# Padded weight tiles in a Mamba-style block: each slot of both projections at another byte offset from its matmul partner

## The reference

```
n    = layernorm(x)
proj = n @ in_proj_w.T               # 512 -> 8192 gates, 8192 hidden, 2*8*128 B and C, 128 dt
hBC  = silu(causal_conv4(hidden, B, C) + conv_b)
dt   = clip(softplus(dt + dt_bias));  A = -exp(A_log)
Y    = chunked state scan over 128 heads of 64, state 128, chunks of 128 tokens, + D * hs
g    = Y * silu(gate);  out = group_rmsnorm(g, 8 groups) * norm_w
x    = x + out @ out_proj_w.T        # 8192 -> 512
x    = x + layernorm(x) @ (W + sum_e probs_e B_e A_e).T + b
```

## The kernel before, in words

|---|---|
| `w_high`, `w_low` and `x_high`, `x_low` (input projection, last product) | 64 |
| `y_high`, `y_low` and `out_high`, `out_low` (output projection) | 0 |
| `wdt_high`, `wdt_low` and `x_high`, `x_low` (dt product of the prologue, L251 to L253) | 192 |
| `y_high` and `x_high` (the one weight load at the switch from L734 to L770) | 352 |

## Time and profile before

### The profile page before, as it was taken

How to read it: one execution, slowest core, us unless ns; L and a number is a source line. 1 busy time by engine, 2 the same in 40 slices (tenths; PEclk the granted TensorE clock), 3 DMA queues, 4 the chain that set the end, 5 groups by cost and what they waited for, 6 DMA issues and landing times.

```text
span 1849.7 us, 32321 instructions
## 1 busy us (share of the span) xinstructions
PE 1693.5 (92%) x9616; PEld 1372.8 (74%) x9616; DVE 1464.4 (79%) x2214; ACT 1186.5 (64%) x1627; POOL 1362.0 (74%) x933
## 2 busy tenths in 40 slices
PE   7789999899998989989899999989999898998989
PEld 4568778687777867777687777867777786777867
DVE  7695986959789595977959689695977959598695
ACT  5674865747667574866658577574856758477562
POOL 1494985949679494985949689494976949588594
PEclk9899999999999999999999999999999999999999
DMA  5542432423344242433434344342433334243231
GB/s 205 198 134 79 159 117 101 132 78 136 107 131 137 83 128 82 154 113 102 136 110 152 102 131 138 94 118 95 140 113 113 123 100 128 89 151 117 94 103 46
DMA packets 121876, 220.40 MB, mean 119 GB/s; under 512 B 30176, under 2 KB 46560, under 8 KB 121312
## 3 DMA queue, kind: packets, MB, share of 16 engines
q1 hardware_dynamic: 121824, 219.76, 37.1%
HBM read 212.88 MB, written 6.82 MB: 119 GB/s over the span
## 4 chain that ended last, share of the span: by engine, by line
POOL 43%; PE 32%; issue 19%; DVE 2%; ACT 1%; POOLq 0%; DVEq 0%; ACTq 0%
POOL w_low L1219 11%; POOL square_sum L1225 8%; POOL scores L1245 8%; POOL xdecay L1264 8%; POOL y L1231 7%; PE bank L770 6%; PE bank L772 6%; PE bank L771 6%; POOL out_low L1254 3%; PE bank L732 3%; PE bank L733 2%; PE bank L734 2%; PE bank L809 1%; PE bank L869 1%; DVE scores L1115 1%
## 5 line engine op out<-in xcount | busy, mean ns | idle before, releaser
L1219 POOL TENSOR_TENSOR w_low<-raw,w_high 128x512 fp32r<-128x512 f32 x285 | 399.6, 1402 | 390.2 <-DVE scores L1115 312.7
L732 PE MATMUL bank<-x_high,w_high 128*128 128x512 f32 x1140 | 484.5, 425 | 6.3 <-POOL w_low L1219 4.1
L733 PE MATMUL bank<-x_low,w_high 128*128 128x512 f32 x1140 | 457.1, 401 | 0.0
L734 PE MATMUL bank<-x_high,w_low 128*128 128x512 f32 x1140 | 455.5, 400 | 0.0
L1019 DVE SCALAR_TENSOR_TENSOR hs<-bank,cols,hs 128x511 f32<-128x511 f32 x381 | 280.7, 737 | 40.1 <-ACT hs L896 40.0
L732 PEld LDWEIGHTS bank<-x_high,w_high 128*128 128x128 f32 x1140 | 219.8, 193 | 73.6 <-issue 31.5
L734 PEld LDWEIGHTS bank<-x_high,w_low 128*128 128x128 f32 x1140 | 218.6, 192 | 53.4
L733 PEld LDWEIGHTS bank<-x_low,w_high 128*128 128x128 f32 x1140 | 220.6, 193 | 41.7
L1033 DVE TENSOR_TENSOR scores<-scores,bc 128x1024 f32<-128x1024 f32 x128 | 242.1, 1891 | 3.7 <-ACT bc L994 3.7
L1264 POOL TENSOR_TENSOR xdecay<-xdt,tables 128x384 f32<-128x384 f32 x128 | 215.7, 1685 | 37.1 <-DVE xdt L1150 37.1
L905 ACT ACTIVATE w_high<-raw 128x512 fp32r<-128x512 f32 x285 | 177.2, 622 | 97.8 <-PE bank L734 90.9
(11 more groups left out here) (135 smaller groups left out, 2933.2 us busy)
## 6 DMA issues: line engine op xcount, KB each, us to landing
raw<-w_in SPq DMA_DIRECT2D x288, 256.0 KB, 2.7
sums<-sums_dram SPq DMA_DIRECT2D x128, 512.0 KB, 3.7
out_raw<-w_out SPq DMA_DIRECT2D x128, 256.0 KB, 3.6
grown_rows<-grown_dram SPq DMA_DIRECT2D x256, 96.0 KB, 3.4
xt<-x SPq DMA_DIRECT2D x8, 256.0 KB, 5.0
mixed<-x SPq DMA_DIRECT2D x2, 1024.0 KB, 7.6
table_dram<-table SPq DMA_DIRECT2D x2, 768.0 KB, 3.7
tables<-table_dram SPq DMA_DIRECT2D x32, 48.0 KB, 2.1
```

The costliest lines, as they stand in the source:

```text
L732: pe.matmul(to[:], w_high[:, slot, k], x_high[:, b, k], start=(k == 0), stop=False)
L733: pe.matmul(to[:], w_high[:, slot, k], x_low[:, b, k], start=False, stop=False)
L734: mm = pe.matmul(to[:], w_low[:, slot, k], x_high[:, b, k], start=False, stop=(k == KT - 1))
L1219: pool.tensor_tensor(w_low[:, t % SPLIT], raw[:, t % RAW], w_high[:, t % SPLIT].bitcast(F32), ALU.subtract).then_inc(w_low_ready, 1)
```

## The change

The tile `w_high` gets 448 bytes in front of it (an unused tile) and 160 bytes of padding behind each of its 3 slots; `w_low` gets 32 bytes in front and the same padding. Each of the 8 slots of `out_high` and `out_low` gets 64 bytes of padding. No instruction is added, removed or moved, and no operand changes its shape; only addresses change. All that is allocated behind `w_low` moves up by 1440 bytes, all behind `out_low` by 2464.

```diff
+W_PAD, OUT_PAD = 40, 16
+W_BASE = (112, 8)
...
-        buffers = (sb("raw", [P, RAW, KT, P]), sb("w_high", [P, SPLIT, KT, P], F32R),
-                   sb("w_low", [P, SPLIT, KT, P], F32R), sb("tap_bc", [P, 2, TAPS + 1]),
+        raw = sb("raw", [P, RAW, KT, P])
+        sb("w_high_base", [P, W_BASE[0]])
+        w_high = sb("w_high", [P, SPLIT, KT * P + W_PAD], F32R)[:, :, 0:KT * P].rearrange("p s (k f) -> p s k f", k=KT)
+        sb("w_low_base", [P, W_BASE[1]])
+        w_low = sb("w_low", [P, SPLIT, KT * P + W_PAD], F32R)[:, :, 0:KT * P].rearrange("p s (k f) -> p s k f", k=KT)
+        buffers = (raw, w_high, w_low, sb("tap_bc", [P, 2, TAPS + 1]),
                    sb("cols", [P, UNITS, TAPS + 3]), sb("hs", [P, H_SLOTS, SEQ]))
...
-        out_high, out_low = sb("out_high", [P, UNITS, HID], F32R), sb("out_low", [P, UNITS, HID], F32R)
+        out_high = sb("out_high", [P, UNITS, HID + OUT_PAD], F32R)[:, :, 0:HID]
+        out_low = sb("out_low", [P, UNITS, HID + OUT_PAD], F32R)[:, :, 0:HID]
```

## The result

In the same series the kernel before took 1850.16 us (median of 20 runs, 1846.98 to 1852.26) and the changed one 1854.44 (20 runs, 1851.52 to 1857.21). The ratio is 1.0022 with a 95% interval of 1.0015 to 1.0029: the change costs about 4 us. The profiled execution of the changed kernel took 1851.84 us at a span of 1850.0, which makes it one of the shortest of its 20 runs; its span is only 0.3 us over the span of before. So this trace must be read by its steps, not by its length.

The account below looks back on a forecast made before the run. POOL was taken to bound the units and PE the step boundaries. Inputs -4.1 us and outputs +5.3 us net +1.2: 1850.9 us on the profiled span of 1849.7, 1851.8 us against the median; range 1834 to 1862.

Parts of the forecast that it names:

- D = 0 was the best place: Rival: output matmuls lose D = 0 in seven of eight slots, giving about 1856 us; chance 0.28.
- signs of being right: Input slot 0 at 226.6 ns, slots 1, 2 below 233; outputs 226.6 to 233; boundary within 0.3 us; unit loop unchanged.
- What bounds the kernel: POOL bounds the units; PE's 48 input and 96 output matmuls at each of 15 step boundaries set the end.
- D matters: Matmul spacing goes with D, the loaded slice's distance within 512 bytes from the streamed one: 226.6 ns at 0, 233.3 at 64.
- D does nothing: Rival: the 6.7 ns between input and output matmuls come from something else, so 1850.6 us; chance 0.10.
- Input side, slot 0: Input matmuls of slot 0 go to D = 0: 6.7 ns less on 408 matmuls, -2.7 us.
- Input side, slots 1 and 2: Input matmuls at D = 160 and 320: 4.4 and 2.3 ns less, -1.0 and -0.4 us; -4.1 us with slot 0.
- the switch: PE's passage from input to output matmuls: seven spacings averaging 231.4 ns, one load at D = 352, taken as 231.
- Output side: Output matmuls leave D = 0 in seven of eight slots: 3.5 ns more on 1524 matmuls, +5.3 us.
- The gain of 17 us: Fast end of the range; any gain over 0.2%, if equal starts were the bad case, had chance 0.32.
- The clock: Steps differ, 111.38 against 109.84 us, with a granted clock of 0.95 in one boundary; unrelated to D, put into the range.
- POOL's addresses: POOL and others read tiles at new starts: taken as 0, between 7 ns either way on some 128 x 6 operations, 3 us.

Follow-up runs that it names:

- experiment 3: Kernel before with w_high and w_low started 448 bytes further on, no slot padded, so D = 0 for all input and output matmuls: 1850.85 us, ratio 0.9998.
- experiment 4: Kernel before with y_high and y_low started 64 bytes further on, no slot padded, so D = 64 for outputs, inputs still 64: 1854.44 us, ratio 1.0019.
- experiment 11: Kernel of experiment 3 with only w_low put at D = 64 (w_high and outputs at D = 0): 1848.76 us in one execution.
- experiment 1: Input padding of the change alone, output tiles unpadded, against the kernel before: 1848.13 us, ratio 0.9986.
- experiment 5: Kernel of experiment 3 with other tile offsets: D = 128 in all input slots, 192 in all output slots: 1851.99 us in one timed execution.
- experiment 9: Kernel before with only raw started 64 bytes further on against w_high and w_low, D unchanged: 1854.47 us, ratio 1.0020.
- experiment 6: Kernel of experiment 3 with other tile offsets: D = 256 in all input slots, 384 in all output slots: 1854.89 us in one timed execution.

## Why the prediction was right, and where its steps were off

The forecast was +1.2 us, 1851.8, with 0.40 on no change beyond 0.2%; measured were +4 us, 1854.44, just over that line and inside the range. The rival that came out is "D = 0 was the best place", at the small end of what it gave. Two things made this look better than it was. The range of 28 us, 1834 to 1862, took in nearly all that was thought likely. And the distance of the forecast from the result is small in part by luck: the steps alone give +6.2 us, five times the forecast sum, and fewer clock stretches, which the forecast could not place, took some 2 us of it back. Of its own signs of being right two did not come: slots 1 and 2 of the inputs stayed at 233, and the boundary grew by 0.38 us and not by less than 0.3; of its signs of being wrong one came, another number of boundaries with a clock below 1.00 (3 for 6).

- **What bounds the kernel**: right. A step changes as its boundary changes; the units hid the slower and the faster matmuls alike.
- **D matters**: right, and "D does nothing" is refuted by experiments 3 and 4. The spacing moves by 6.7 ns of 227 at a granted clock of 1.00 with nothing but an address changed. That the load of the next weights takes the time from the running matmul is not shown: in experiment 11 the matmul under which `w_low` is loaded is not the one that takes long (228.7 ns, against 235.1 for the `w_low` matmul itself).
- **Input side, slot 0**: right, 226.7 ns once settled. But the next step's x tile, which follows output matmuls at 232 ns, took about six matmuls to settle and gave 4.4 ns a matmul, not 6.7.
- **Input side, slots 1 and 2**: wrong. I took 228.9 for D = 160 "nearest to the 192 row" and 231 for 320 from the switch. Both stayed at 233.3. The term of -4.1 us was about -1.5 (experiment 1: 15 steps x 0.10).
- **Output side**: the sign right, the size short. The step that was off is the interpolation between D = 0, 192 and 352: it gave 3.5 ns a matmul, measured are 4.9 in the first block (232.1 against 227.2 over all its 47 spacings, rows 932.79 and 943.70 here, 932.59 and 943.27 in the earlier trace rows). Spacing does not go smoothly with D; it has one good value at 0 and 256 (226.7 to 227 ns) and one bad one, 232 to 233, at nearly all the others read. The weak reading at 352 was no reading of a distance but of matmuls that had not settled. The 228.9 of the dt product was one of two rhythms that D = 192 can have (experiment 5), and I had read it as a property of the distance.
- **The sum of these**: +0.41 us a step, 6.2 us in 15, where the forecast had +1.2 in all. Of the last step's output matmuls 72 lie on the chain and not 84, since two groups of 12 were made before 1801.80 and not one; this changes the sum by less than 0.1 us.
- **The gain of 17 us at the fast end of the range**: not shown by any run. Even with all 816 input matmuls at 226.6 (5.5 us) it needs the 1524 output matmuls at 219 ns, and the shortest settled spacing at a granted clock of 1.00 in any trace is the 226.6 or 226.7 of D = 0.
- **The clock**: right as a disturbance, and larger than the two clock stretches in the range, which are 3.1 us by the earlier trace rows (111.38 against 109.84 us for a step with one) and 3.2 by the windows above. The steps alone would have made the change 6 us and experiment 4 8 us longer; the medians say 4 and 3. In the profiled executions the missing part is fewer stretches at the boundaries. The runs without a profile fit this, since their granted clock is higher too (0.9745 and 0.9755 against 0.972), but that their boundaries are where it was gained is argued, not shown. Why a kernel with longer steps has fewer boundaries with a stretch at a granted clock of 0.50 stays open.
- **POOL's addresses**: I took 0 with a bound of 7 ns. In the changed kernel it is nearly so (mean 1406 ns against 1402). But the bound came from two lines that both had all their operands at equal starts, and so could not show what unequal starts can cost: 14 ns (experiments 3 and 9), enough to eat 0.19 us a step, most of the gain of the input side.

## What to carry to other kernels

Before padding SBUF tiles, work out from the tile sizes where each pair of operands stands, and read the spacing of the same matmul at each distance the trace already has; equal starts modulo 256 bytes were the good case here (226.7 ns against 233), and spreading the slots took it away. Move the one tile that brings the pair together without parting others: moving x gained 0.29%, moving the weights, which also stand in POOL's subtraction, gained nothing. A reading of one stretch is not yet the cost of an address, since operands at the same distance can settle at two spacings (228.8 and 233.2 ns at D = 192).

## What the runs showed that was not expected

- At a granted clock of 1.00, matmuls of 512 columns in fp32r came every 226.7 ns at D = 0, 227 at 256, and 232 to 233 at 32, 64, 128, 160, 320, 384 and 480; one element of 4 bytes off was enough (232 ns). At D = 16 some tiles settled at 227 and some at 233. At D = 192 two blocks of the same step ran at 228.8 and 233.2 ns. At 0.50 they came every 426.7 or 426.8 ns at D = 0, 16, 64, 256 and 480.
- The spacing has a memory: a tile at D = 0 behind matmuls at D = 0 runs at 226.7 ns from its start (experiment 1), behind others at 228.9 on average over 12 (the changed kernel). So the effects of two changes of addresses did not add.
- The 128x512 subtraction of L1219 on POOL took 1399 to 1408 ns on average in the traces of ten kernels and 1414 to 1418 in those of experiments 3, 6 and 9, by where its operands lie against each other, with the same instruction and neighbours.
- A boundary that catches a stretch at a granted clock of 0.50 was 1.6 us longer (37.44 against 35.85), and their number (1 to 7 of 15 in the profiled executions of all kernels) is worth up to 9 us, more than the effects studied. It is not the only source of a spread between runs: of two profiled executions of experiment 9's kernel, 1850.4 and 1855.2 us long, the second has its first marked wait 3.4 us later (193.55 against 190.15), and only one boundary with at most one stretch lies before it. The step without such a stretch showed them more clearly than medians of 8 to 20 runs.
